# Sets of two batches for the experts: a Trainium2 kernel of three transformer blocks, one core

## What is computed

```python
x = L0_attn_x
x = x + 0.5 * ffn(layernorm(x))          # stage 0
x = x + attention_with_bias(layernorm(x))  # stage 1, "mid"
x = x + 0.5 * ffn(layernorm(x))          # stage 2

def ffn(x):
    x = x + msa(ln(x, ln1_w, ln1_b))      # softmax attention, 16 heads
    return x + moe(ln(x, ln2_w, ln2_b))

def moe(x):                               # one expert per token
    logits = xf @ gate_w + gate_b
    one_hot = jax.nn.one_hot(jnp.argmax(logits, axis=-1), E)
    h = gelu(jnp.einsum('td,edh->teh', xf, w1))
    y = jnp.einsum('teh,ehd->ted', h, w2)
    return jnp.einsum('te,ted->td', one_hot, y)
```

## Time and profile before

| | |
|---|---|
| median of 3 runs | 2529.06 us (2525.1 to 2532.25) |
| profiled execution | 2526.46 us, span 2524.6 us |
| granted TensorE clock, mean | 0.956 |
| busy: PE / DVE / ACT / POOL | 91% / 78% / 79% / 32% |
| DMA | 278.80 MB, mean 110 GB/s |
| first exponential of step 0 | 72.7 us |

### The profile page before, as it was taken

One profiled execution on the slowest core, in us unless ns is written; L12 is line 12 of the kernel. 1 busy time (PEld: TensorE's weight loads), 2 busy tenths in 40 slices (PEclk: granted clock), 3 DMA queues, 4 the chain that ended last, 5 costly groups with the idle time before them and its releaser, 6 DMA issues.

```text
span 2524.6 us, 63176 instructions
## 1 busy us (share of the span) xinstructions
PE 2297.1 (91%) x24460; PEld 880.3 (35%) x24460; DVE 1957.8 (78%) x3260; ACT 1982.1 (79%) x3604; POOL 810.4 (32%) x1083
## 2 busy tenths in 40 slices
PE   4898887988999999999999999999999999999945
PEld 1232223422532543453333333332222442532535
DVE  7987895697689679668889889889999779689310
ACT  1797776886989977877778778788988989988922
POOL 1462432344262261322433302312232042241252
PEclk7899888997999999999999999999999999999967
DMA  5345436434423744745445444321221512612535
GB/s 152 96 153 145 79 79 170 140 93 118 126 81 94 201 128 112 187 120 162 108 129 148 110 135 109 88 58 36 69 50 49 158 43 58 167 41 57 144 88 134
DMA packets 322308, 278.80 MB, mean 110 GB/s; under 512 B 79212, under 2 KB 267436, under 8 KB 321976
## 3 DMA queue, kind: packets, MB, share of 16 engines
q1 hardware_dynamic: 310744, 266.37, 39.0%
q0 software_dynamic: 11264, 8.40, 1.9%
HBM read 202.91 MB, written 84.02 MB: 114 GB/s over the span
## 4 chain that ended last, share of the span: by engine, by line
PE 59%; DVE 18%; DMA 6%; issue 6%; SPq 5%; ACT 3%; POOL 3%; POOLq 0%; DVEq 0%
PE psum L1028 20%; DVE maxes L1314 13%; PE psum L963 11%; PE psum L990 9%; PE psum L1146 4%; PE psum L1011 4%; PE psum L1157 4%; ACT probs L1210 3%; DMA neg_max<-max_parts 2%; SPq L518 2%; DVE biased L1319 2%; PE psum L1081 2%; DMA q_staged<-neg_max 1%; DMA m_y<-sorted_tokens 1%; PE psum L1087 1%
## 5 line engine op out<-in xcount | busy, mean ns | idle before, releaser
L1210 ACT ACTIVATE probs<-psum 128x512 f32<-128x512 f32 x3072 | 1657.7, 598 | 317.9 <-PE psum L990 177.9
L1314 DVE TENSOR_REDUCE maxes<-psum 128x2 f32<-128x1024 f32 x1216 | 1429.1, 1215 | 292.4 <-PE psum L963 290.2
L1028 PE MATMUL psum<-probs,v_ones 128*9 128x256 f32 (+1 forms) x11520 | 947.9, 401 | 0.0
L963 PE MATMUL psum<-k_staged,q_staged 48*128 48x512 bf16 x3072 | 613.8, 396 | 86.4 <-DVE maxes L1314 60.8
L990 PE MATMUL psum<-q_staged,k_staged 51*128 51x512 bf16 (+1 forms) x3072 | 631.9, 384 | 37.1 <-DMA q_staged<-neg_max 21.0
L1319 DVE CUSTOM_DVE_ANT_0 biased<-psum,strips 128x512 bf16<-128x512 f32 x640 | 411.5, 686 | 99.1 <-PE psum L963 93.4
L963 PEld LDWEIGHTS psum<-k_staged,q_staged 48*128 48x128 bf16 x3072 | 147.8, 93 | 757.7 <-DVE maxes L1314 409.0
L750 POOL CAST max_parts<-max_turned 128x32 bf16<-128x32 f32 x96 | 20.3, 212 | 1020.8 <-DVE max_turned L1357 1020.8
L990 PEld LDWEIGHTS psum<-q_staged,k_staged 51*128 51x128 bf16 (+1 forms) x3072 | 258.4, 95 | 196.4 <-ACT probs L1210 62.0
L1028 PEld LDWEIGHTS psum<-probs,v_ones 128*9 128x9 f32 x11520 | 171.1, 88 | 386.9 <-issue 297.6
L1011 PE MATMUL psum<-near,ident_b 64*64 64x256 bf16 (+4 forms) x3840 | 149.3, 251 | 0.0
(11 more groups left out here) (150 smaller groups left out, 1386.5 us busy)
## 6 DMA issues: line engine op xcount, KB each, us to landing
m_w<-in_w SPq DMA_DIRECT2D x240, 256.0 KB, 3.4
near<-bias_near SPq DMA_DIRECT2D x128, 240.0 KB, 4.4
q_staged<-q_parts SPq DMA_DIRECT2D x96, 192.0 KB
k_staged<-k_parts SPq DMA_DIRECT2D x96, 192.0 KB
strips<-bias_strips SPq DMA_DIRECT2D x64, 288.0 KB, 3.4
q_parts<-p_part SPq DMA_DIRECT2D x23, 384.0 KB
k_parts<-p_part SPq DMA_DIRECT2D x23, 384.0 KB
bias_cuts<-bias_window SPq DMA_DIRECT2D x32, 240.0 KB, 3.5
```

The lines of the kernel that those rows point to most:

```text
L963: last = pe.matmul(slots[at % 2][:, s, :], k.qst[u % STAGED][rows_, i, qtile * P:(qtile + 1) * P], k.kst[u % STAGED][rows_, i, chunk * HAL ...
L1028: last = pe.matmul(heads_bank[32 * j:32 * j + VC, columns], k.v[:, batch_of(u) * KT + kt, u % QUADS * 4 + j, :], probs[:, step % 3 * 4 + j ...
L1210: act.activation(probs[:, step % 3 * 4 + e % 4, :], bank[:, :], ACT.Exp).then_inc(taken, 1)
L1314: dve.reduce_max(maxes[u % 2][:, half, 2 * i:2 * i + 2, t, chunk], slot, AX.X).then_inc(drained, 1)
```

## The change

- Sets of two batches. `BATCHES` puts batches 0 and 1 of stage 0 in a set, 2 and 3 of stage 0, 0 and 1 of stage 2; batches 2 and 3 of stage 2 stay alone. A set of two has 16 + 7 = 23 tiles in 8 trips, 3 steps apart, first at route + 28; a set of one has 5 trips, 4 steps apart, as before. `MT` is 24. Routing buffers are twice as wide. Sets of two are routed after their second batch: at 149, 277 and 661.
- The 14 place operations come four a step in four steps.
- Scatters: one a step over 16 steps for a set of two. Gathers: two a step over four steps, at route + 54 for the first batch and + 86 for the second.
- Tokens: two buffers `m_y`, loaded two trips ahead.
- Strips: a DMA now writes 8 rows of all 16 heads, each row one run of 9 * 128 bf16 values; before, a DMA wrote 128 rows of one head in eight pieces each.
- `NEAR_STEPS` are 61, 85, 109, 125.
- Sums of the heads are inverted, stored and loaded one step later, and GpSimd's product with them too.
- `project_step` of stage 1 is gather_step + 6h + 18 (before + 8h + 16), of stage 2 output_step(1, b, 1) + 8h + 72 (before + 16).
- q and k of units 16 and 24 (`LATE_UNITS`) are loaded all together, two steps after the store of the second half, at steps 238 and 366.
- The zeros of each sorted buffer are written by two DMAs of 12 tiles, before by one of 15.

```diff
-MT = KT + E - 1
+MT = 2 * KT + E
-SETS = [(n, b) for n in (0, 2) for b in range(B)]
+BATCHES = {(0, 0): (0, 1), (0, 2): (2, 3), (2, 0): (0, 1), (2, 2): (2,), (2, 3): (3,)}
+SETS = list(BATCHES)
+SET_OF = {(n, b): (n, first) for (n, first), batches in BATCHES.items() for b in batches}
+def trips(n, b):
+    return -(-(len(BATCHES[n, b]) * KT + E - 1) // SLOTS)
...
+FIRST_TRIP = {1: 26, 2: 28}
+SCATTER = {1: (13, 14, 15, 16, 17, 18, 19, 20), 2: tuple(range(10, 26))}
+GATHER = (0, 0, 1, 1, 2, 2, 3, 3)
+def trip_step(n, b, trip):
+    return route_step(n, b) + FIRST_TRIP[len(BATCHES[n, b])] + (3 if len(BATCHES[n, b]) == 2 else 4) * trip
+def gather_step(n, b):
+    key = SET_OF[n, b]
     if (n, b, 1) in LAST:
-        return trip_step(n, b, TRIPS - 1) + 8
-    return route_step(n, b) + 8 * (WINDOWS + 3)
+        return trip_step(*key, trips(*key) - 1) + 8
+    if len(BATCHES[key]) == 1:
+        return route_step(*key) + 8 * (WINDOWS + 3)
+    return route_step(*key) + 54 + 32 * BATCHES[key].index(b)
...
-        return gather_step(0, b) + 8 * h + 16
-    return output_step(1, b, 1) + 8 * h + 16
+        return gather_step(0, b) + 6 * h + 18
+    return output_step(1, b, 1) + 8 * h + 72
...
-NEAR_STEPS = [8 * w + 5 for w in (WINDOWS + 3, WINDOWS + 5, WINDOWS + 7, 2 * WINDOWS + 3)]
+NEAR_STEPS = [8 * w + 5 for w in (WINDOWS - 1, WINDOWS + 2, WINDOWS + 5, WINDOWS + 7)]
...
+LATE_UNITS = [(B + b) * QUADS for n, b in SETS if n == 0]
...
-    def shear_strip(sp, quad, piece):
-        run, j = STRIP // 8, piece
-        sp.dma_start(k.strips[quad][:, j, :].rearrange("p (o c) -> o p c", o=8), bass.AP(
-            k.strip_dram.tensor, (quad * 4 + j) * RELS + P + STRIP_AT, [[run, 8], [-1, P], [1, run]])
-                     ).then_inc(strips_cut, 16)
+    def shear_strip(sp, piece):
+        rows_ = P // (QUADS * STRIP_CUTS)
+        p = piece * rows_
+        sp.dma_start(k.strips[:, p:p + rows_, :], bass.AP(
+            k.strip_dram.tensor, P + STRIP_AT - p, [[RELS, H], [-1, rows_], [1, STRIP]])).then_inc(strips_cut, 16)
...
-            if step == first - 4:
-                load_tokens(sp, n, b, 0)
...
+            for trip in range(2):
+                if step == first - 3 + trip:
+                    load_tokens(sp, n, b, trip)
+            count = trips(n, b)
+            for trip in range(count):
+                if step == trip_step(n, b, trip) + 1 and trip + 2 < count:
+                    load_tokens(sp, n, b, trip + 2)
+                if step == trip_step(n, b, trip) + 2 and trip + 2 < count:
+                    for r in range(SLOTS):
+                        load_w1(sp, n, b, trip + 2, r)
...
-            if 5 <= since < 12:
-                dve_place(dve, n, b, (since - 5) * 2 + i)
+            if 5 <= since < 9:
+                for op in range(((since - 5) * 2 + i) * 2, min(((since - 5) * 2 + i) * 2 + 2, 14)):
+                    dve_place(dve, n, b, op)
...
-                    if u + 2 < UNITS and t in UNIT_LOADS:
+                    for late in LATE_UNITS:
+                        if step == project_step(1, batch_of(late), 1) + STORE_SINCE + 2:
+                            for piece in range(len(UNIT_LOADS)):
+                                load_unit(sp, late, piece)
+                    if u + 2 < UNITS and u + 2 not in LATE_UNITS and t in UNIT_LOADS:
```

More of the change, by code:

```diff
@@ L70 @@
 SLOTS = 3
-TRIPS = MT // SLOTS
-assert TRIPS * SLOTS == MT
 OUTPUTS = [(n, b, h) for n in range(STAGES) for b in range(B) for h in range(2)]
-SETS = [(n, b) for n in (0, 2) for b in range(B)]
+BATCHES = {(0, 0): (0, 1), (0, 2): (2, 3), (2, 0): (0, 1), (2, 2): (2,), (2, 3): (3,)}
[3 more added lines that the diff above has]
+    return -(-(len(BATCHES[n, b]) * KT + E - 1) // SLOTS)
+assert all(trips(n, b) * SLOTS <= MT for n, b in SETS)
+TRIP_KEYS = [(n, b, trip) for n, b in SETS for trip in range(trips(n, b))]
 LAST = [(STAGES - 1, B - 1, h) for h in range(2)]
@@ L141 @@
 LAST_STEP = gather_step(2, B - 1) + 8
-DOWN_STEPS = {trip_step(n, b, trip) + 2: [(n, b, trip)] for n, b in SETS for trip in range(TRIPS)}
+DOWN_STEPS = {trip_step(*key) + 2: [key] for key in TRIP_KEYS}
+LATE_UNITS = [(B + b) * QUADS for n, b in SETS if n == 0]
 class Core:
@@ L246, in taken_places @@
                 put("r_count", n, b)
-            for trip in range(TRIPS):
+            for trip in range(trips(n, b)):
                 since = step - trip_step(n, b, trip)
@@ L386, in trip_index, with set_tiles, moved_tiles, wait_gathered @@
     def trip_index(n, b, trip):
-        return set_index[n, b] * TRIPS + trip
+        return TRIP_KEYS.index((n, b, trip))
     def trip_key(done):
-        return (*SETS[done // TRIPS], done % TRIPS)
+        return TRIP_KEYS[done]
+    def set_tiles(n, b):
+        return len(BATCHES[n, b]) * KT
+    def moved_tiles(at):
+        return sum(set_tiles(*SETS[i]) for i in range(at % 2, at + 1, 2))
+    def wait_gathered(engine, n, b):
+        at, i = set_index[SET_OF[n, b]], BATCHES[SET_OF[n, b]].index(b)
+        sets = [s for s in range(at % 2, at + 1, 2) if len(BATCHES[SETS[s]]) > i]
+        engine.wait_ge(gathered[at % 2][i], len(sets) * KT * 16)
+    def zn_tiles(n, b, h):
+        first = BATCHES[SET_OF[n, b]].index(b) * KT + h * 4
+        return range(first, first + 4)
+    def zn_before(n, b):
+        at, i = set_index[SET_OF[n, b]], BATCHES[SET_OF[n, b]].index(b)
+        return (SETS[at - 1][0], BATCHES[SETS[at - 1]][i]) if at else None
     def split_tiles(n, b, h):
@@ L477, in store_zeros @@
         for p in range(2):
-            sp.dma_start(k.sorted[p].rearrange("(t p) c -> p t c", p=P),
-                         zeros.rearrange("p (t c) -> p t c", c=C)).then_inc(stored, 16)
+            for part_ in range(2):
+                sp.dma_start(k.sorted[p].rearrange("(o t p) c -> o p t c", o=2, p=P)[part_],
+                             zeros.rearrange("p (t c) -> p t c", c=C)).then_inc(stored, 16)
     def pace(sp, step):
@@ L1103, in pe_norm_turn @@
         pe.wait_ge(o_normed, ffn_index[n, b, h] + 1)
-        for t in range(4):
-            last = pe.transpose(bank[:, t * P:(t + 1) * P], zn[:, h * 4 + t, :], k.ident[:, :])
+        for t, tile in enumerate(zn_tiles(n, b, h)):
+            last = pe.transpose(bank[:, t * P:(t + 1) * P], zn[:, tile, :], k.ident[:, :])
         last.then_inc(scored, 1)
@@ L1280, in act_between @@
                 bank = take(act, "r_count", n, b)
-                act.activation(counts[:, :], bank[:, 0:(KT + 1) * E], ACT.Copy).then_inc(taken, 1)
-            for trip in range(TRIPS):
+                size = (set_tiles(n, b) + 1) * E
+                act.activation(counts[:, 0:size], bank[:, 0:size], ACT.Copy).then_inc(taken, 1)
+            for trip in range(trips(n, b)):
                 since = step - trip_step(n, b, trip)
```

220 lines of the change are left out of this document (111 added, 109 removed).

## The result

The changed kernel takes 2491.56 us (median of 4 runs, 2487.09 to 2492.45), the kernel before 2530.28 us beside it: 0.985 of it, 95% interval 0.983 to 0.987. It is 39 us faster. Forecast were 85 us: the sign was right, the time lies 47 us above the forecast and 9.6 us above the range.

What follows compares the result with a forecast made beforehand. The prediction took TensorE as the bound, its attention pieces back to back without slack. Its terms summed to -84.5 us from the profiled 2526.5, giving 2442.0; with 2.6 for the median, 2444.6 us, range 2415 to 2482.

Steps and rivals of the forecast that it cites:

- 1. trips: Expert trips: 34 instead of 40, at 5.7 us each, all counting on TensorE: -34 us.
- 2. near loads in their new place: Stage 0, steps 52 to 59 and 116 to 123: near loads keep 7 of 74 us of stalls; -67 us.
- 5. late q and k: Units 16 and 24: TensorE waits for late-loaded q and k, +7 and +2.5, together +9.5 us (0 to +16).
- 6. gathers beside outputs: Steps 203 and 715: gathers on GpSimd delay an output's sum and norm, +2.8 us twice, +5.6 (0 to +12).
- 7. projections in stage 2: Two projections move from the middle stage to stage 2: -1 us.
- 7. first tokens: First tokens of two-batch sets load right after the last scatter, behind a carry: +2 us in all (0 to +6).
- 7. routing: VectorE's routing: three sets in the stages vanish, three are twice as wide, four operations a step: +2 us (-4 to +6).
- rival C: SP can't feed a trip every 3 steps: 1.5 us each on 24 trips, +36, 2481 us; chance 0.10.
- Rival A: Near copies in stage 0 hit row maxima at steps 67, 91, 115, 131: +12 us on average, 2457; chance 0.12.
- Rival B: Stage 0's stall moves, with SP loaded at steps 52 to 59; half of 74 us returns: +30, 2475; chance 0.15.
- Rival D: New waits of items 5 and 6 don't show, units and stores landing sooner: -15 to -20, 2427 us; chance 0.09.
- Rival E: Slower than before, 2540 us: SP falls behind in trip stretches, so the carry of the maxima comes late; chance 0.04.

Runs made afterwards that it cites:

- a_old_near: Changed kernel with the near copies back at steps 93, 109, 125, 157: 2516.6 us, 0.993 of the kernel before.
- a_late2: Changed kernel, stage 1 projections 5 steps apart instead of 6, their GpSimd norms queued 5 steps ahead instead of 7: 2482.85 us, 0.980 of the kernel before.
- a_gather: Changed kernel, second four gathers of a two-batch set's batch five steps after the first, that batch's store four steps later: 2489.16 us, 0.982.
- a_project: Changed kernel, last batch's projections for stage 2 at steps 547 and 555 instead of 595 and 603: 2496.0 us, 0.985.
- a_tokens: Changed kernel, first tokens of one-batch sets loaded a step earlier, ahead of the carry of the maxima: 2495.73 us, 0.985.
- b_strips: Kernel before with only the strips by 8 rows of all heads: 2516.36 us, 0.992.
- a_again: The changed kernel measured once more, without edits: 2497.54 us, 0.986 of the kernel before.
- b_place4: Kernel before with only the 14 place operations four a step in four steps, instead of two a step in seven: 2543.56 us, 1.0035.
- a_old_strips: Changed kernel with the old strip shears, 128 rows of one head in eight pieces each: 2516.33 us, 0.993 of the kernel before.

## Why the prediction was wrong

The forecast of the span was 2524.6 - 84.5 = 2440.1 us; it is 2489.8. The 49.7 us by the steps of the prediction:

| step of the prediction | forecast | measured | miss |
|---|---|---|---|
| 1. trips | -34 | -27: the two pairs of units with eight trips, 126.9 and 127.9, less 79.6 for units 35 and 36, which have none, are 5.9 and 6.0 us a trip, not 5.7 | +7 |
| 2. near loads in their new place | 7 of 74 left | 15: 7.8 in units 3 and 4 (`a_old_near`), about 7.3 in units 7 and 8, 86.9 against 79.6 for units 35 and 36 | +8 |
| 5. late q and k | +9.5 | +15.0 (`a_late2`) | +5.5 |
| 6. gathers beside outputs | +5.6 | +21: unit 13 51.2 against 40.1 before, unit 45 52.3 against 42.4; `a_gather` gave 10.8 of it back | +15 |
| 7. projections in stage 2 | -1, no wait | wait of 6.8 in unit 37 (`a_project`) | +7 |
| 7. first tokens | +2, sets of two only | 5.1 more for the sets of one (`a_tokens`) | +5 |
| 7. routing | +2 | about +7: units 9, 17 and 41 43.5, 48.2, 43.5 against 40.0 (unit 5), 46.8 and 41.1 (before) | +5 |
| 3, 4. tail, start | -5, +3.4 | -3.1 (119.8 to 116.7), +2.9 | +1.4 |

The misses sum to 54 against 49.7; the rest is within the scatter of the units named above. For the trips and the routing the cause is argued from the windows; no run tests them in the changed kernel.

What was right. The strips no longer hold SP, and without the near loads their units are clean (41.7 and 41.6 us in `b_strips`, 41.5 and 41.6 in `a_old_near`). In the changed kernel no routing operation takes over 0.5 us. The trips at three steps apart are fed; rival C's 1.5 us each were 0.3. Rival A (copies meet a row maximum) didn't come: no row maximum of stage 0 took over 0.35 us, and none lay under a near copy (those nearest to the second four began at 366.11 and 385.11 us, the copies last from 369.43 to 383.72). Rival B was right in its mechanism and far too large in its price: the near loads push the carry back. At step 127 the parts of the maxima are done at 406.4 us, SP takes them up only at 412.91, and that step takes 9.2 us. Rival D, that the new waits don't show, was the opposite of what happened. Rival E never came near.

Where it failed. Items 5 and 6 found the right waits and priced each at its own length; what follows a wait was put at nothing, without a reason. Item 6 is the largest miss. Its order of events and its chain were right: from the first exponential of step 203 (657.4 us) to the end of the norm (685.7) it is 28.3 us, forecast 27.7. The term beside it was wrong: "some 25 us of steps" were 21.9. So the wait was not 2.8 but 5.0 us at TensorE's gate in unit 13, and 5.2 in unit 45. And a wait of 5.0 us cost 11. Step by step against the kernel before, 5.8 of the 11.0 us lie in the long step (8.7 against 2.9), 3.6 in the two steps behind it (5.7 and 3.2 against 3.1 and 2.2), and the rest is spread over the unit, in which a part of a projection now lies too. In the first of the two steps the granted clock was 0.50, with TensorE busy all the time (a window of all engines: TensorE, its weight loads, VectorE, ScalarE and GpSimd, each with its busy time and count, then the granted clock, DMA share and GB/s):

```profile
687.90:693.60 5.70, 5.70 (x36) 2.32 (x40) 3.74 (x12) 2.37 (x5) 2.37 (x7) 0.50 0.02 2
```

In `a_project` and `a_again` the wait is the same 5.0 us and the long step the same 8.7; in the first the next steps take 4.3 and 2.2 us and the unit 48.7, at a mean granted clock of 0.93, in the second 5.7, 3.9 and 3.0 and the unit 52.6, at 0.87. The granted clock read 0.50 for 6.8 us in the first (686.0 to 692.8) and for 13.7 in the second (689.4 to 703.1), 10.2 in the profile of the changed kernel above. So up to 4 us of the price go with the length of this stretch; what sets its length, no run shows.

For item 5 the waits were 6.1 and 5.0 us, forecast 7 and 2.5. The way from the turn of the maxima to the landed q and k was 24.4 us in unit 15 and 24.2 in unit 23, forecast 23. TensorE came to that place 18.3 and 19.2 us after the turn, forecast 15.5 and 20.5, so in the middle stage the longer steps gave less than booked. The units lost 7.4 and 7.6 us by these waits. In unit 37 TensorE waited 4.4 us, and the unit lost 6.8.

Then, two waits were not looked for. The projections moved by 56 steps were booked as bare work, without their norm on GpSimd, which landed ahead of an output's sum. For the first tokens only the sets that were new were checked, not the single ones, whose load moved behind a carry too.

The range was too narrow in the same way: it took B or C to be the one large loss, and seven smaller misses of 5 to 15 us, all of one sign, made it instead.

## What to carry to other kernels

When a schedule without slack is moved, list for each moved operation the in-order engine it now stands on and the next thing behind it that TensorE needs; the meetings found here cost 5 to 11 us each. Book a new wait at more than its own length: those measured here cost 1.2 to 2.2 times theirs. A change in parts is to be judged in company: two parts that brought 16 and 12 us alone cost 21 to 22 each when undone, and the last 33 us came from five small moves in the order.

## What the runs showed of the hardware

A GpSimd copy held VectorE operations with two SBUF inputs (3.79 us for 0.216 in the earlier trace rows, 2.16 us for L1568 in `b_place4`), and not these alone: in `b_place4` also a scalar operation of 15 columns (3.41 us) and a cast of 15 columns (4.74 us), each to the end of the copy, and a cast of 24 columns took the same 4.74 us in `a_old_near`, 0.18 in the changed kernel. A maximum from PSUM took its usual 1.22 us under a copy in `b_place4`, a reduction of 64 columns (L1562) its usual 0.20 us under one in the kernel before. Other work of GpSimd held an operation too: in the kernel before a row maximum, also with two SBUF inputs and 0.165 us in the median, took 1.93 us from 728.16 and ended with a product of GpSimd (2.13 us from 727.94). What makes one operation held and another not, no run shows.

The price of a DMA of short runs fell on the next issue of the same queue: in unit 3 of `a_old_strips` 0.63 to 0.69 us for the strip of 1024 runs of 288 bytes, 2.17 to 3.70 us for the load behind it. With 128 runs of 2304 bytes, the same bytes, the changed kernel took 0.53 to 0.56 us for the strip there and 0.59 or 0.60 for the load.

Waits of TensorE cost more than their length here: in unit 13 a wait of 5.0 us was followed by a step of 5.7 us at a granted clock of 0.50, and the unit took 8.6 to 12.5 us more than in the kernel before.
